# Two transformer layers on one core: row factors by GpSimd, x updated by ScalarE, and score products of one VectorE operation a block

## What is computed

```python
x = x + attention0(ln(x))      # 16 heads of 16, no mask
x = x + gated_lora(ln(x))      # 8 experts, the best one per token
x = x + attention1(ln(x))      # causal, 16 heads, 4 key/value groups
x = x + moe(ln(x))             # 32 experts of width 128, top 4, and a shared one

def gated_lora(x):             # x is the normalized row here
    x_diff = x - select_mean_diff[n];  x_diff = x_diff / norm(x_diff)
    score  = sum((select_weight[n] @ x_diff) ** 2)
    gate   = sigmoid(slope[n] * (score - center[n]))
    s, i   = gate.max(), gate.argmax()                     # over the 8 n
    return (1 - s) * x + s * (bias[i] + degen[i] @ (update[i] @ (x - debias[i])))
```

## Time and profile before

| | us |
|---|---|
| median of 3 runs (range) | 689.49 (688.66 to 690.69) |
| the profiled execution | 689.53 |
| its span, first to last instruction | 687.7 |
| PE / DVE / ACT / POOL busy in the span | 568.5 / 463.7 / 349.7 / 241.9 |
| mean granted TensorE clock | 0.921 of full |

### The profile page before, as it was taken

One profiled execution on the slowest core, in us unless ns is written; L12 is line 12 of the kernel. 1 busy time (PEld: TensorE's weight loads), 2 busy tenths in 40 slices (PEclk: granted clock), 3 DMA queues, 4 the chain that ended last, 5 costly groups with the idle time before them and its releaser, 6 DMA issues.

```text
span 687.7 us, 14444 instructions
## 1 busy us (share of the span) xinstructions
PE 568.5 (83%) x4178; PEld 401.2 (58%) x4179; DVE 463.7 (67%) x1347; ACT 349.7 (51%) x906; POOL 241.9 (35%) x318
## 2 busy tenths in 40 slices
PE   4998998998796789788878789744667999989995
PEld 2664564564586554656556566523455788767774
DVE  4578786883278882847695863665658777767764
ACT  1532765778475546155744555422014666556563
POOL 2433000014120133345434343547503555545540
PEclk9999799999998899989989997977659999999999
DMA  7598789000000018584005161144223445444589
GB/s 236 195 312 247 219 228 280 3 4 3 1 1 2 0 59 244 173 239 184 4 14 207 40 225 41 54 177 164 87 90 110 142 150 154 142 130 144 152 326 355
DMA packets 49534, 95.20 MB, mean 138 GB/s; under 512 B 8580, under 2 KB 40524, under 8 KB 46924
## 3 DMA queue, kind: packets, MB, share of 16 engines
q1 hardware_dynamic: 41804, 75.34, 35.6%
q0 software_dynamic: 7680, 19.21, 7.4%
HBM read 58.54 MB, written 35.59 MB: 137 GB/s over the span
## 4 chain that ended last, share of the span: by engine, by line
PE 50%; DVE 24%; DMA 7%; ACT 6%; issue 6%; POOL 2%; another core or an unknown queue 2%; SPq 1%; DVEq 0%; ACTq 0%; POOLq 0%
PE banks L1524 9%; PE banks L1321 6%; PE banks L1535 5%; PE banks L1277 4%; PE banks L1147 4%; PE banks L1342 3%; DVE mx L1836 3%; DMA arena<-negT 3%; PE banks L1513 2%; PE banks L1153 2%; DVE mx L1839 2%; DMA arena<-results_by_rank 2%; PE banks L1222 2%; PE banks L1436 2%
## 5 line engine op out<-in xcount | busy, mean ns | idle before, releaser
L1015 ACT ACTIVATE arena<-banks 128x512 f32<-128x512 f32 (+1 forms) x256 | 130.2, 547 | 92.3 <-PE banks L1321 57.7
L1321 PE MATMUL banks<-arena 98*128 98x256 bf16 (+1 forms) x512 | 91.4, 274 | 29.4 <-DVE arena L1939 10.2
L868 POOL DMA_INDIRECT results_by_rank<-attn_w,goes x80 | 77.2, 965 | 90.0 <-issue 45.2
L1836 DVE TENSOR_REDUCE mx<-banks 128x4 f32<-128x1024 f32 x64 | 76.1, 1220 | 19.8 <-PE banks L1277 19.8
L1277 PE MATMUL banks<-arena 96*128 96x256 bf16 (+1 forms) x512 | 85.2, 271 | 3.8 <-DVE mx L1836 2.4
L1524 PE MATMUL banks<-arena,attn_w 128*128 x320 | 84.8, 389 | 0.4 <-issue 0.3
L833 POOL DMA_INDIRECT rows_by_expert<-arena,bpb x64 | 63.1, 987 | 55.6 <-ACT arena L1015 34.2
L1321 PEld LDWEIGHTS banks<-arena 98*128 98x128 bf16 x512 | 44.6, 103 | 65.0 <-ACT arena L1015 17.2
L1839 DVE TENSOR_REDUCE mx<-banks 128x4 f32<-128x1024 f32 (+1 forms) x48 | 58.1, 1222 | 28.9 <-PE banks L1281 28.6
L1277 PEld LDWEIGHTS banks<-arena 96*128 96x128 bf16 x512 | 51.4, 102 | 20.6 <-DVE mx L1836 5.1
L1524 PEld LDWEIGHTS banks<-arena,attn_w 128*128 128x128 f32 x320 | 55.8, 195 | 5.7 <-issue 1.2
(11 more groups left out here) (239 smaller groups left out, 1134.5 us busy)
## 6 DMA issues: line engine op xcount, KB each, us to landing
arena<-parts_dram SPq DMA_DIRECT2D x72, 256.0 KB, 4.2
pvs<-rows_by_expert SPq DMA_DIRECT2D x80, 130.0 KB
parts_dram<-arena SPq DMA_DIRECT2D x24, 384.0 KB, 3.6
arena<-results_by_rank SPq DMA_DIRECT2D x6, 1024.0 KB, 10.2
arena<-in SPq DMA_DIRECT2D x2, 2304.0 KB
rows_by_expert<-zero SPq DMA_DIRECT2D x1, 4160.0 KB, 23.8
arena<-in SPq DMA_DIRECT2D x2, 1920.0 KB
arena<-in SPq DMA_DIRECT2D x3, 768.0 KB
```

The lines of the kernel that those rows point to most:

```text
L868: pool.indirect_dma_start(ys, bass.IndirectOffsetOnAxis(ap=goes[:, j:j + 1], axis=0), yb[j], None).then_inc(y_stored[j], 16)
L1015: act.activation(p_ring[n][:, i % P_RING, :], st_bank[RING_AT[n]["s", b, s] % 3][:, 0:P_WIDTH[n]], ACT.Exp, scale=HD ** -0.5).then_inc(exp ...
L1321: ins = pe.matmul(dst[:, at:at + SEQ - q0], keys, q_rows(n, slice(0, ROWS), s, b, q0, SEQ - q0), start=True, stop=(n == 0 or b < POOL_MASKS))
L1836: ins = dve.tensor_reduce(out, src.rearrange("p (q h k) -> p q h k", q=QT, k=nk), AX.X, ALU.max)
```

## The change

In the middle, POOL works out xx from numbers it has: a row with variance v and rstd r has the square sum 256·v·r² after the norm (three small products behind shift, stage B). ACT's square sums are gone. The update x += keep·xn1 becomes x = (1 + keep·rstd)·x + keep·shift: POOL makes both factors (stage D, three small operations), ACT applies them one tick later (stage E, four activations at the end of its tick), and DVE's addition in stage F waits for that. DVE's update and its clamp before the exponential are gone (the clamp is now part of an operation behind it). ACT takes the exponential between the second and the third tile of the norm of that tick. In the expert loop DVE has 40 blocks written out in place of 8; one operation on one tile (a product or a sum) stands behind each of 32 steps, and the weights follow after step 39.

```diff
+LEADING = 2 * TILES // 4 + 2
...
             def scale(stage, c):
-                pool.tensor_tensor(rstd[:, at], var[:, at], mhalf[:, :], ALU.pow).then_inc(pool_norm, 1)
-                pool.wait_ge(pool_norm, i + 1)
+                then(pool.tensor_tensor(rstd[:, at], var[:, at], mhalf[:, :], ALU.pow))
                 pool.tensor_tensor(shift[:, at], nmean[:, at], rstd[:, at], ALU.mult).then_inc(norm_ready, 1)
+                if stage == "B":
+                    then(pool.tensor_tensor(xx[:, at], rstd[:, at], rstd[:, at], ALU.mult))
+                    then(pool.tensor_tensor(xx[:, at], xx[:, at], mv[:, at, 1], ALU.mult))
+                    pool.tensor_tensor(xx[:, at], xx[:, at], width[:, :], ALU.mult).then_inc(squares_ready, 1)
+            def scale_kept(c):
+                pool.wait_ge(keep_found, c + 1)
+                pool.wait_ge(norm_ready, NORM_STAGES.index(("B", c)) + 1)
+                then(pool.tensor_tensor(row_scale[:, at], keep[c % 2][:, :], rstd[:, at], ALU.mult))
+                pool.tensor_tensor(row_shift[:, at], keep[c % 2][:, :], shift[:, at], ALU.mult)
+                pool.tensor_tensor(row_scale[:, at], row_scale[:, at], ones[:, 0:CT], ALU.add).then_inc(keep_scaled, 1)
...
             def normalize(stage, c, dst, ready, gated):
-                if dst is xn2[1] and c == 1:
-                    act.wait_ge(squares_ready, TILES)
                 if ready is xn1_ready and c >= 3:
-                    act.wait_ge(kept, c - 2)
+                    act.wait_ge(job_ready[1], JOBS1.index((c - 3, "TC1")) + 1)
                 for t in range(CT):
...
+                    if t == 1 and gated is not None:
+                        gate_exp(gated)
+            def add_kept(c):
+                act.wait_ge(keep_scaled, c + 1)
+                for n in range(c * CT, (c + 1) * CT):
+                    ins = act.activation(x[:, n, :], x[:, n, :], ACT.Identity, bias=row_shift[:, n:n + 1],
+                                         scale=row_scale[:, n:n + 1])
+                ins.then_inc(kept, 1)
-            def squares(c):
-                    act.activation(junk[:, t, :], xn1[c % 3][:, t, :], ACT.Square,
-                                   accum_out=xx[c % 2][:, t:t + 1]).then_inc(squares_ready, 1)
...
             def gate(c):                       # DVE
-                step(1, dve.tensor_tensor(s3, s2, col(slob), ALU.mult))
-                dve.tensor_scalar(s0, s3, -80.0, None, ALU.max).then_inc(logit_ready, 1)
+                dve.tensor_tensor(s3, s2, col(slob), ALU.mult).then_inc(logit_ready, 1)
                 dve.wait_ge(gate_exp_ready, c + 1)
-                step(1, dve.tensor_scalar(s2, s1, 1.0, None, ALU.add))
+                step(1, dve.tensor_scalar(s2, s1, FINITE, 1.0, ALU.min, ALU.add))
...
-                for t in range(CT):
-                    rows = x[:, c * CT + t, :]
-                    ins = dve.scalar_tensor_tensor(out=rows, in0=xn1[c % 3][:, t, :], scalar=keep[p][:, t:t + 1], in1=rows,
-                                                   op0=ALU.mult, op1=ALU.add)
-                ins.then_inc(kept, 1)
...
-            for b in range(1, 8):
-                dve_step_moe(b, b % 2, b % 4, b, stored=16 if b == 7 else None)
-                if 3 * (b - 1) < TILES:
-                    score_product(3 * (b - 1), min(3 * b, TILES))
+            for b in range(1, 4 * LEADING):
+                dve_step_moe(b, b % 2, b % 4, b, stored=(b - 3) // 4 * 16 if b >= 7 else None)
+                t, second = divmod(b - 1, 2)
+                if t < TILES and second:
+                    score_sum(t)
+                elif t < TILES:
+                    score_product(t)
...
-            with dve.Fori(2, trips) as i:
+            with dve.Fori(LEADING, trips) as i:
```

More of the change, by code:

```diff
@@ L319, in two_block_kernel @@
                      for at, size in ((0, FW), (CT * FW, NSEL * SELW), (CT * (FW + NSEL * SELW), MW)))
-        xx, top, least, keep = ([sb(f"{name}{i}", [P, CT]) for i in range(2)] for name in ("xx", "top", "least", "keep"))
+        top, least, keep = ([sb(f"{name}{i}", [P, CT]) for i in range(2)] for name in ("top", "least", "keep"))
+        xx, row_scale, row_shift = (sb(name, [P, TILES]) for name in ("xx", "row_scale", "row_shift"))
+        width = sb("width", [P, CT])
         sc = [[sb(f"sc{n}_{i}", [P, CT, NSEL]) for i in range(4)] for n in range(2)]
@@ L759, in _, with then @@
             pool.tensor_copy(identb[:, :], ident[:, :]).then_inc(constants_made, 1)
+            pool_steps = [5]
+            def then(ins):
+                pool_steps[0] += 1
+                ins.then_inc(pool_step, 1)
+                pool.wait_ge(pool_step, pool_steps[0])
             for j in range(len(SPLIT0)):
@@ L804, in _ @@
             for tick in range(TICKS):
-                for stage, c in wave(tick, "FBH"):
+                for stage, c in wave(tick, "FBHD"):
                     if stage == "H":
                         low(c)
+                    elif stage == "D":
+                        scale_kept(c)
                     else:
@@ L1044, in _ @@
                             turn_copy(c, f"T{stage}{k}", turned["ACG".index(stage)][:, k, :])
-                for stage, c in wave(tick, "FBHDC"):
+                gated = dict(wave(tick, "D")).get("D")
+                last_norm = [stage for stage, c in wave(tick, "FB")][-1:]
+                for stage, c in wave(tick, "FBHE"):
                     if stage == "F":
-                        normalize("F", c, xn2[c % 2], xn2_ready)
+                        normalize("F", c, xn2[c % 2], xn2_ready, gated if last_norm == ["F"] else None)
                     elif stage == "B":
-                        normalize("B", c, xn1[c % 3], xn1_ready)
+                        normalize("B", c, xn1[c % 3], xn1_ready, gated)
                     elif stage == "H":
                         middle(c)
-                    elif stage == "D":
-                        gate_exp(c)
                     else:
-                        squares(c)
+                        add_kept(c)
             wait_saved(act, 1, range(len(SPLIT1)))
```

43 lines of the change are left out of this document (22 added, 21 removed).

## The result

The changed kernel takes **677.65 us** (median of 4 runs, 675.67 to 680.5). Beside it the kernel before took 689.08 (median of 4). The ratio is **0.9854** [0.9816, 0.9892], so the gain of 1.5% is clear of the noise; the time is 1.7 us under the forecast of 679.3 and inside its range. The profiled execution took 677.33, its span is 675.5 us (before 687.7), and the mean granted clock is 0.929 (before 0.921).

A forecast was written before the change was run, and what follows sets the result against it. DVE bounds the middle's 10.97 us ticks; DVE's chain, then PE, bounds the expert loop. From 689.5, minus 8.0 for the middle and 2.2 net for the loop, gives 679.3 us, range 674.5 to 684.5.

The forecast's parts named there:

- A tick of 10.97 becomes 9.3: Middle, ticks 4 to 6: earlier exponential and DVE's removed update, less a wait for ACT, save 1.67 us each.
- ACT's update ends last by 0.6: Middle, from tick 4: DVE is ready at +5.3, ACT's updates end at +5.9, so DVE's addition waits about 0.6 us.
- PE takes over at tick 7, second projection at 242.0, 5.46 us long: Middle: PE becomes the bound, and its second Q, K, V projection starts at 242.0 in place of 249.33.
- The 1.2 us of clock: Middle, second projection: without standing for DVE, PE may keep the upper clock level and give 1.2 us more.
- The cover of POOL's additions and of the removed squares: Middle: POOL's added 0.8 us costs nothing, removed ACT squares gain nothing; about 4 us cover the later norm for PE.
- The expert loop's start: First expert blocks: PE sets the pace from the third block; gain 2.5 to 5.4 us, taken as 4.0.
- The entry at block 40: Expert loop: weights and DVE's loop entry, 1.95 us, meet 0.5 slack a block; loss 1.8 us, 1.0 to 3.0.
- Instruction loads move: A DVE stall of up to 4.7 us vanishes (674.6) or a second comes (684.0); one in eight each.
- No wait for kept: Middle: ACT's updates pack closer, ticks 4 to 6 save 2.3 us each, middle gives 9.4; 677.9, one in ten.
- POOL blocks DVE: Middle: new POOL operations hold up DVE's gate through a shared port, costing 3.6 us; 682.9, one in twenty-five.
- DVE becomes the bound: Expert loop: small operations keep DVE's step at 2.31 us for 32 blocks, 17.6 later; 699, one in fifty.
- The entry costs all: Expert loop: DVE's loop entry takes back all the first blocks gained, net 0; 681.5, one in ten.

The follow-up runs named there:

- exp_only: Kernel before, with only ACT's exponential between second and third norm tile and the clamp ahead of it gone; ratio 0.997 to the kernel before, tick 10.24 us.
- late_exp: Changed kernel with the exponential put back behind all four norm tiles; ratio 0.989 to the kernel before, tick 9.39 us.
- experts_only: Kernel before, with only the expert-loop part of the change; ratio 0.998 to the kernel before.
- after_again: The changed kernel unaltered, run again on another chip; ratio 0.983 to the kernel before.
- mid_only: Kernel before, with only the middle part of the change and the old expert loop; ratio 0.990 to the kernel before.
- pool_busy: Changed kernel plus eight extra POOL products behind each three square-sum products, beside DVE's gate; ticks 9.33 and 9.25 us, one run.
- trips_early: Changed kernel with DVE's loop trip count loaded before the first block instead of behind step 39; ratio 0.978 to the kernel before.
- weights_spread: Changed kernel with the four weight operations spread behind steps 33 to 36 instead of all behind step 39; ratio 0.981 to the kernel before.
- loads_early: Changed kernel with weight operations spread over steps 33 to 36 and trip counts loaded before the first block on DVE, ACT and PE; ratio 0.986 to the kernel before.
- three_tiles: Changed kernel, but DVE does product and sum of three tiles behind each of 32 steps; blocks 2 to 32 take 65.2 us in place of 52.3.

## Why the prediction was right, and where it was not

**A tick of 10.97 becomes 9.3: right**, 9.24 to 9.25. Every point of it was within 0.1 us, tick 3 too (additions 8.06 apart in place of 10.40: 2.3 saved, as forecast).

**ACT's update ends last by 0.6: right**, 0.51. What the working hides, and exp_only and late_exp show, is how the credit falls: the update alone is worth 1.6 a tick, the exponential alone 0.73, both together 1.72.

**PE takes over at tick 7, second projection at 242.0, 5.46 us long: right** in this execution (242.38, 5.46). The nearness of 242.38 is in part luck: the middle started 0.93 later than before, and counted from its start the projection came 0.5 earlier than forecast. The sum had PE's transposes and down products at 3.7, and they took 3.1 from start to start; it also took the old start of the second projection as 249.33, where the earlier trace rows has 249.12. The 1.2 us of clock are a chance, not a term: in 4 of the 11 traces with the new middle one of the first two projections took 6.6 to 7.2, and the third came 1.4 to 2.0 later than in the five that show it earliest (66.7 to 67.0). In all three traces with DVE's update of x (before, experts_only, exp_only) one of the two took 6.7 to 6.9. Whether the new middle makes this rarer, three traces can't tell. With the old middle the third projection came at 74.4 and 75.8, so the middle's gain lies between 5.7 and 9.2 us, and the forecast's 8.0 in it.

**The cover of POOL's additions and of the removed squares: right.** None shows on the path. ACT's last update ends at 247.44 (forecast 247.0), and PE does not stand for the norm behind it.

**Attention 1: missed.** The prediction's sum had nothing there, and 3.4 us came. They are 0.9 of a transfer and then PE's clock. In the kernel before, the transfer of the second row of maxima took 6.04 us, and in three stretches of 3 us from 301.93 on (it ended at 303.24) the granted clock was 0.63, 0.50 and 0.73; in the first profile of the changed kernel it took 5.10, and the clock stayed at 1.00. But kernels with the same program up to there differ as much. Busy time by stretch (columns as in the earlier trace rows) right behind that wait, after_again and then mid_only:

```profile
293.99:296.99 3.00, 2.98 (x41) 2.26 (x42) 0.99 (x2) 1.80 (x5) 1.17 (x3) 1.00 0.73 225
296.99:299.99 3.00, 2.49 (x35) 1.73 (x33) 2.86 (x8) 1.48 (x4) 1.61 (x4) 1.00 0.89 233
```

```profile
295.36:298.36 3.00, 2.08 (x22) 1.10 (x22) 0.28 (x1) 1.26 (x3) 1.08 (x3) 0.68 0.76 229
298.36:301.36 3.00, 3.00 (x29) 2.29 (x26) 1.27 (x2) 1.10 (x4) 0.50 (x2) 0.75 0.92 238
```

Clock 1.00 in the one, 0.68 and 0.75 in the other, and 25.4 against 27.9 us between the first and the third row of maxima. With the new middle this stretch takes 25.4 to 29.5, with DVE's update of x 25.9, 27.0 and 29.6: nothing that the change can be given. What goes with it is how long PE stood for that transfer. In the eight traces in which it took 4.3 to 5.2 us, the clock behind it stayed at 1.00 and the third row of maxima came 15.9 to 16.8 us after the second; in the six in which it took 5.4 to 6.0, that was 17.5 to 20.4, and in five of them the first 3 us behind it ran at 0.50 to 0.62 (pool_busy, 5.91, kept 1.00). Both groups have kernels with either middle. So 3.4 of the 12.2 us were luck of one profile, and the median, 1.7 us under the forecast, may owe something to it.

**The expert loop's start: right**, 4.0 forecast, 3.9 measured in the first profile, 4.3 to 5.5 on the two chips that had both. One figure in it was off: DVE's own step is 1.12, not 1.21. It mattered only for the slower rival.

**The entry at block 40: right in size, the slack too small.** Forecast a loss of 1.8 (1.0 to 3.0), measured 1.1 to 1.8. I took it as DVE time that meets a slack, 1.95 − 0.5, so each part should give back its length. trips_early gave 1.2 for at most 1.04 of issue, which leaves nearly nothing for the weights to cost alone; weights_spread gave 0.2 for 0.9, with 1.07 lost to one slow load of a block. The slack is then nearer 0.8, an estimate: either part alone costs 0.1 to 0.2, both together 1.1.

**Rivals.** *Instruction loads move*, one in four: fell in both directions. The long waits stand at the same instructions of DVE and ACT in before, after and loads_early, whatever was added or taken away ahead of them, and nowhere on three other chips. *No wait for kept* and *POOL blocks DVE*: fell, the latter with the remainder that pool_busy shows. *DVE becomes the bound*: three_tiles shows it would have cost 13, not 17.6. *The entry costs all*: no.

## What to carry to other kernels

When two edits shorten two lines that end nearly together, price them together: the second is worth only what the first leaves, here 0.14 in place of 0.73 us a tick. Load a loop's trip count well before the loop: at the entry DVE stood 1.04 us in issue, most of it this load, and moving it ahead of the first block gave 1.2 back. And read a stage's time from several traces before a microsecond or two behind a standing PE is explained: with the same instructions ahead, one stretch of attention 1 took 25.4 us in one execution and 29.5 in another.

## What was not expected of the hardware

The same kernel takes 671 to 674 us on some chips and 688 to 689 on others. Between the third row of maxima and the first block of the experts lie about 11 of these 17 us (192.8 to 193.6 against 179.2 to 185.0), and in this stretch are the waits of DVE and ACT on nothing of the kernel (4.7 to 4.8, 3.7 to 5.3, 2.9), at fixed instructions. Some 4.5 are in the late blocks (65.1 against 60.6 us for blocks 44 to 79, after and after_again), where a single step takes 3.7 to 4.3. What the waits are was not found out.

Beside elementwise work on POOL some of DVE's operations take 0.03 to 0.18 us longer, two with a single tensor operand among them, and others with two SBUF operands no longer than before (pool_busy).

The longer PE stood for the transfer of the second row of maxima, the likelier was the lower clock behind it: none of eight traces with 4.3 to 5.2 us, five of six with 5.4 to 6.0.
